# Linear attention in chunks of 64 tokens, with the state carried twice per tile and the query-value product in two banks by turns

## The chip, the cores and the metric

One Trainium2 chip, one of its cores. The metric is the device time of one execution in microseconds (us).

## The reference

Two layers in float32 on X of 2 x 2048 tokens with 256 channels, each added to its input. The first is a linear attention with 16 heads of 16 channels; the second a mixture of 32 experts with a shared one.

```python
K = X.reshape(B, L, H, d)                       # X is the normalised input
Q = rms_norm_multihead((X @ Wq.T).reshape(B, L, H, d), q_norm_w)
V = rms_norm_multihead((X @ Wv.T).reshape(B, L, H, d), v_norm_w)
W = jnp.cumsum(jnp.einsum('blhd,blhe->blhde', K, V), axis=1)
out = jnp.einsum('blhd,blhde->blhe', Q, W)      # token l sees all tokens up to l
# second layer: softmax over 32 experts, the best 4 of each token, swiglu of each, plus a shared swiglu
```

## The kernel before

The tokens are 32 tiles of 128, on 128 partitions. The kernel has three stages. The attention stage (about 20 to 215 us) computes the attention and, some tiles behind, the second norm, the routing and the scatter of the tokens to their experts. The expert stage (about 260 to 495 us) takes 144 blocks of tokens one after the other, and the end gathers and adds. The change is in the attention stage; in the part between the stages only banks of the shared expert's matmuls change places.

Each engine has its own program, unrolled by `pipelined(n, depth, step)`: iteration i calls `step`, and inside it `tile_of(s)` is tile i - s, so that the order of the statements in `step` is the order of that engine's instructions, with tiles of several ages mixed. Semaphores by name join the engines; `wait(eng, S[name], count)` blocks everything behind it on that engine.

What TensorE does for tile t, with its lines:
- L774 transposes the routed layer's input of an older tile, L785 the normalised input `xn` of a new one (into `xnT`), both into the bank `pT0`.
- L828 is the query-value product, `xnT` with `wqv`, 512 columns in two steps, into the bank `pQV`. ScalarE squares it (L571), VectorE sums, ScalarE and VectorE make the root (L594, L602, L1191 to L1216), and VectorE writes the normed queries `qn` (L1234) and values `vp` (L1240). The next product waits for both, since there is one bank.
- L817 transposes `qn` into `pT0`; ScalarE copies it as `qm` (four copies, L556) and `qT` (L562).
- L795 makes the scores: for each of 2 halves of the channels and each of 4 row groups of 32 channels, keys of 128 tokens against 256 columns (two heads' masks by 128 queries), into the four banks `pS`. VectorE multiplies three banks by the triangle `tri` (L1089), ScalarE copies the fourth (L527) and GpSimd cuts its triangle (L482).
- L869 is the product of the queries with the state `w_bd` carried from earlier tiles, a block-diagonal matrix, into `pO`. L877 adds the tile's keys and values to the state in `pT1`; VectorE writes it back as `w_bd` (L1180), once per tile. L888 adds the product of the masked scores with the values to `pO`. These three have 32 columns of weights each, in the four column groups.
- ScalarE scales `pO` into `oT` (L614), L803 transposes it, VectorE adds it to `xall` (L1113) and takes the statistics for the second norm.
- L838, L846, L847 and L858 belong to the routing and run every second tile.

GpSimd scatters the rows of a tile with four indirect DMAs (L467); SP's queue zeroes `ys` (L358) meanwhile.

Of the kernel before, what the change touches and what calls it, by code (L numbers as in the profile page):

```python
# [51 lines left out]
def build(nc, X, Wq, Wv, q_norm_w, v_norm_w, Wg, W1, W2, W3, Ws1, Ws2, Ws3, out):  # L52
# [12 lines left out]
    HB = P // 2  # L65
    NM = E // 2
# [21 lines left out]
    def banks_copied(t):  # L88
        return t

    def banks_masked(t):
        return 3 * t
# [25 lines left out]
    with ctx:  # L118
# [93 lines left out]
        s_sb = part(2048).rearrange("p (j g r l) -> p j g r l", j=4, g=2, r=2)  # L212
# [5 lines left out]
        xn = part(3 * 256).rearrange("p (b c) -> p b c", b=3)  # L218
# [43 lines left out]
        def tab_part(rows, width):  # L262
# [30 lines left out]
        pS = [pb(f"pS{j}") for j in range(4)]  # L293

        early = {(1, 0, 0): pQV, (1, 0, 1): pO, (1, 1, 0): pT1, (1, 1, 1): pS[0], (2, 0, 0): pS[2], (2, 0, 1): pS[1],
                 (2, 1, 0): pS[3], (2, 1, 1): pT1, (3, 0, 0): pS[2], (3, 0, 1): pS[3],
                 (3, 1, 0): pT0, (3, 1, 1): pQV}

        def h_bank(g, m, n):
# [5 lines left out]
            qn_done v_done qT_ps qm_done qT_done state_ps state_done scores_ps masked o1_ps o_ps oT_done  # L305
# [5 lines left out]
            xT_ps xT_done hb_ps sge_done ge_done gT_ps gT_done y_ps y_done parts_sum parts_copied half_sum added summed s_copied masked_pool padded w13_staged w2_staged y2_done kept""".split()  # L311
# [14 lines left out]
        DVE_CONSTS = 20  # L326
# [86 lines left out]
        def _(pool):  # L413
# [56 lines left out]
            def step(tile_of):  # L470
                if (a := tile_of(9)) is not None:
                    pool_wait(S["xr_done"], a.t + 1)
                    pool_wait(S["prob_done"], a.p + 1)
                    pool_wait(S["dest_done"], a.t + 1)
                    pool_wait(S["pos_done"], a.p + 1)
                    scatter(a, 0)
                if (a := tile_of(9)) is not None:
                    scatter(a, 1)
                if (a := tile_of(2)) is not None:
                    pool_wait(S["s_copied"], banks_copied(a.t) + 1)  # L480
                    v = s_sb[:, 1].rearrange("p g r l -> p (g r) l")
# [23 lines left out]
        def _(act):  # L505
# [3 lines left out]
            def normalise(t):  # L509
# [6 lines left out]
                wait(act, S["state_ps"], t - 2)  # L516
                act.activation(xn[:, t % 3, :], xall[:, t, :], ACT.Identity, bias=bias, scale=scale).then_inc(S["xn_done"], 1)
# [6 lines left out]
            def copy_scores(a, j):  # L524
                wait(act, S["scores_ps"], 4 * a.t + j + 1)
                wait(act, S["o_ps"], a.t)
                act.copy(s_sb[:, j].rearrange("p g r l -> p (g r l)"), pS[j][:]).then_inc(S["s_copied"], 1)  # L527

            def step(tile_of):
                if (a := tile_of(1)) is not None:  # L530
                    wait(act, S["xnT_ps"], a.t + 1)
                    wait(act, S["scores_ps"], 4 * (a.t - 2))
# [16 lines left out]
                if (a := tile_of(3)) is not None:  # L549
                    copy_scores(a, 1)  # L550
                if (a := tile_of(2)) is not None:
                    wait(act, S["qT_ps"], a.t + 1)
                    wait(act, S["scores_ps"], 4 * a.t)
                    for r in range(2):
                        for g in range(KC):
                            last = act.activation(qm[:, r, g, :], pT0[:, g * P:(g + 1) * P], ACT.Copy,  # L556
                                                  scale=mwq[:, r, g:g + 1])
                    last.then_inc(S["qm_done"], 1)
                if (a := tile_of(2)) is not None:
                    wait(act, S["qT_ps"], a.t + 1)  # L560
                    wait(act, S["o1_ps"], a.t - 1)
                    act.copy(qT[:, a.b], pT0[:, 0:D].rearrange("p (g m) -> p g m", g=KC)).then_inc(S["qT_done"], 1)  # L562
                if (a := tile_of(5)) is not None:
                    wait(act, S["nb2_done"], a.t + 1)
                    wait(act, scattered[a.r8], 64 * (a.t // 8))
                    act.activation(xr[:, a.r8, 0:D], xall[:, a.t, :], ACT.Identity, bias=nb[:, a.b, 0:1],
                                   scale=rr[:, (a.t + LAG) % 2, 2 * H:2 * H + 1]).then_inc(S["xr_done"], 1)
                if (a := tile_of(1)) is not None:
                    wait(act, S["qv_ps"], a.t + 1)
                    wait(act, S["ss_done"], a.t)  # L570
                    act.activation(sq, pQV[:], ACT.Square, scale=float(d) ** -0.5).then_inc(S["sq_done"], 1)  # L571
# [14 lines left out]
                if (a := tile_of(0)) is not None and a.t > 1:  # L586
                    normalise(a.t)
# [20 lines left out]
                if (a := tile_of(3)) is not None:  # L608
                    wait(act, S["o_ps"], a.t + 1)
                    wait(act, S["ot_ps"], a.t)  # L610
                    if a.t == 0:
                        act.wait_ge(S["wc_in"], 64)
                    for g in range(KC):
                        last = act.activation(oT[:, g, :], pO[:, g * P:(g + 1) * P], ACT.Copy, scale=wvc[:, g:g + 1])  # L614
                    last.then_inc(S["oT_done"], 1)
# [105 lines left out]
        def _(pe):  # L721
# [38 lines left out]

            def step(tile_of):
                if (a := tile_of(5)) is not None:
                    if a.t == NT - 3:
                        pe.wait_ge(S["masked"], banks_masked(NT))
                        pe.wait_ge(S["s_copied"], banks_copied(NT))
                        shared_half(0, 0, 0)
                    wait(pe, S["xr_done"], a.t + 1)
                    wait(pe, S["qT_done"], a.t + 4, NT)
                    wait(pe, S["qm_done"], a.t + 4, NT)
                    wait(pe, S["lg_done"], (a.t - 1) // 2)  # L770
                    wait(pe, S["rk_done"], (a.t - 2) // 2)
                    wait(pe, S["lgT_done"], a.t // 2)
                    for c in range(KC):
# [4 lines left out]
                    if a.t == NT - 1:  # L778
                        shared_half(0, 1, 1)
                if (a := tile_of(0)) is not None:  # L780
                    wait(pe, S["xn_done"], a.t + 1)
                    wait(pe, S["qT_done"], a.t - 1)
                    wait(pe, S["qm_done"], a.t - 1)
                    for g in range(KC):
                        last = pe.transpose(pT0[:, D + g * P:D + (g + 1) * P], xn[:, a.r3, g * P:(g + 1) * P], ident[:])  # L785
                    last.then_inc(S["xnT_ps"], 1)
                if (a := tile_of(2)) is not None:
# [3 lines left out]
                    wait(pe, S["masked"], banks_masked(a.t))  # L791
                    wait(pe, S["s_copied"], banks_copied(a.t))
                    for g in range(KC):
                        for j in range(4):
                            last = pe.matmul(pS[j][:, g * 256:(g + 1) * 256], xnT[32 * j:32 * j + 32, a.r3, g, :],  # L795
                                             qm[32 * j:32 * j + 32, :, g, :], start=(g == 0), stop=True,
                                             skip_group_check=True)
                            if g == KC - 1:
                                last.then_inc(S["scores_ps"], 1)
                if (a := tile_of(3)) is not None:  # L800
                    wait(pe, S["oT_done"], a.t + 1)
                    for g in range(KC):
                        last = pe.transpose(pO[:, D + g * P:D + (g + 1) * P], oT[:, g, :], ident[:])  # L803
                    last.then_inc(S["ot_ps"], 1)
                    if a.t == NT - 2:
                        pe.wait_ge(S["state_done"], NT - 1)
                        shared_half(1, 1, 0)
                    if a.t == NT - 1:
                        shared_half(0, 0, 1)
# [667 lines left out]
```

## Time and profile before

| | us |
|---|---|
| median of 3 runs | 559.55 (555.07 to 562.66) |
| the profiled execution | 559.33 |
| its span, first to last instruction | 557.4 |
| TensorE busy | 527.4 |
| VectorE, ScalarE, GpSimd busy | 382.2, 376.5, 331.8 |

The rows of the profile come from the one profiled execution. "Busy" is the time in which an engine has at least one instruction in work; TensorE's matmuls overlap each other, so their durations add up to more than the time that they take. PE is TensorE's matmuls, PEld its weight loads, DVE VectorE, ACT ScalarE, POOL GpSimd. A float32 matmul of the program is two matmul records and two weight loads in the trace.

### The profile page before, as it was taken

To read this page: it belongs to the slowest core of one execution; us is meant where nothing else is said; L and a number is where in the kernel's file an instruction comes from. 1 tells how busy PE (TensorE), PEld (TensorE's weight loads), DVE (VectorE), ACT (ScalarE), POOL (GpSimd) and SP (SyncE) were. 2 spreads that over 40 slices of the span, in tenths; PEclk is the share of its full clock that TensorE was granted. 3 is DMA by queue.
4 is the path that set the end of the run, shared out by engine and by line. 5 is a ranking of instruction groups with operands and counts; after the bars stand their busy time and mean duration, and the time that the engine had idled before them with its cause. 6 is when DMAs were issued, how large, how long until landed. Compare 5 with 4: busy or idle time off the path is not lost.

```text
span 557.4 us, 18176 instructions
## 1 busy us (share of the span) xinstructions
PE 527.4 (95%) x5177; PEld 383.1 (69%) x5177; DVE 382.2 (69%) x1354; ACT 376.5 (68%) x1258; POOL 331.8 (60%) x367
## 2 busy tenths in 40 slices
PE   6798999999999999699999999999999999997996
PEld 2355666666666665357998988999999995544554
DVE  7698999999999996664444444444444446744786
ACT  2687899988989985402766766777677776653452
POOL 6010377776777777771665555666666564446992
PEclk8999999999999999899999999999999999998999
DMA  8998355556456554954676776766666554428999
GB/s 259 316 292 264 125 217 211 187 215 227 186 198 246 188 192 152 366 194 127 195 219 201 221 225 199 214 193 194 194 193 198 180 187 145 143 79 342 408 409 347
DMA packets 65088, 123.29 MB, mean 221 GB/s; under 512 B 9824, under 2 KB 44000, under 8 KB 64992
## 3 DMA queue, kind: packets, MB, share of 16 engines
q1 hardware_dynamic: 47824, 78.07, 44.1%
q0 software_dynamic: 13056, 39.86, 19.2%
q10 hardware_dynamic: 4112, 4.19, 2.3%
q8 instruction: 45, 0.74, 0.6%
q14 instruction: 51, 0.42, 0.3%
HBM read 58.49 MB, written 63.60 MB: 219 GB/s over the span
## 4 chain that ended last, share of the span: by engine, by line
PE 79%; DMA 5%; DVE 4%; issue 4%; ACT 3%; POOL 2%; SPq 1%; ACTq 1%; DVEq 0%; POOLq 0%
PE pS L967 18%; PE pQV L828 10%; PE pS L985 9%; PE pS L741 8%; PE pS L795 5%; PE pO L888 5%; DMA xg<-xs 3%; PE pO L869 3%; PE pT L946 3%; PE pQV L946 2%; PE pQV L757 2%; PE pO L757 2%; PE pT L774 2%; PE pO L803 2%; PE pT L817 1%
## 5 line engine op out<-in xcount | busy, mean ns | idle before, releaser
L495 POOL DMA_INDIRECT ys<-gsh,dst x144 | 138.1, 959 | 108.3 <-ACT gsh L663 86.6
L467 POOL DMA_INDIRECT xs<-xg,posi x128 | 123.8, 967 | 52.1 <-issue 31.4
L967 PE MATMUL pS<-after_a,x2T_all 128*128 128x128 f32 x1024 | 135.5, 276 | 0.0
L967 PEld LDWEIGHTS pS<-after_a,x2T_all 128*128 128x128 f32 x1024 | 124.5, 192 | 0.0
L1375 DVE TENSOR_TENSOR after_a<-after_a,pS 128x128 f32<-128x128 f32 x144 | 41.5, 288 | 79.9 <-ACT after_a L651 76.1
L1346 DVE COPY x2T_all<-w 128x512 f32 x144 | 63.9, 444 | 32.9 <-issue 32.5
L985 PE MATMUL pS<-w,after_a 128*128 x256 | 76.7, 381 | 0.0
L1089 DVE TENSOR_TENSOR w<-pS,tri 128x512 f32<-128x512 f32 x96 | 65.1, 679 | 1.0 <-PE pS L795 1.0
L828 PE MATMUL pQV<-w 128*128 128x512 f32 x128 | 63.7, 621 | 0.5 <-ACT w L533 0.5
L663 ACT ACTIVATE gsh<-pS,xg 128x256 f32<-128x256 f32 x128 | 60.6, 474 | 0.4 <-issue 0.4
L662 ACT CAST dst<-xg 128x1 int32 x128 | 24.5, 191 | 45.3 <-PE pS L985 43.3
L741 PE MATMUL pS<-x2T_all,ws 128*128 128x512 f32 x104 | 50.6, 636 | 1.3 <-ACT sg L624 0.7
L651 ACT ACTIVATE after_a<-pS 128x128 f32<-128x128 f32 x144 | 40.1, 279 | 16.5 <-PE pS L967 10.7
L482 POOL TENSOR_SCALAR_AFFINE_SELECT w<-w 128x512 f32<-128x512 f32 x32 | 20.6, 643 | 43.3 <-ACT w L527 43.0
L500 POOL TENSOR_TENSOR w<-w 128x512 f32<-128x512 f32 x32 | 40.7, 1272 | 7.7 <-DMA w<-ys 7.4
L985 PEld LDWEIGHTS pS<-w,after_a 128*128 128x128 f32 x256 | 38.9, 192 | 0.4 <-issue 0.4
L556 ACT ACTIVATE w<-pT,mwq 128x128 f32<-128x128 f32 x128 | 36.8, 379 | 1.9 <-PE pT L817 1.7
L741 PEld LDWEIGHTS pS<-x2T_all,ws 128*128 128x128 f32 x104 | 20.9, 207 | 24.6 <-issue 24.3
L795 PE MATMUL pS<-w 32*128 32x256 f32 x512 | 36.7, 401 | 0.0
L828 PEld LDWEIGHTS pQV<-w 128*128 128x128 f32 x128 | 22.2, 194 | 20.2 <-issue 18.2
L888 PE MATMUL pO<-w 128*32 128x128 f32 x1024 | 34.6, 274 | 1.3 <-POOL w L482 0.6
L647 ACT COPY after_a<-pT 128x256 f32<-128x256 f32 x72 | 26.1, 363 | 11.4 <-PE pT L946 11.3
(221 smaller groups left out, 1019.8 us busy)
## 6 DMA issues: line engine op xcount, KB each, us to landing
xg<-xs SPq DMA_DIRECT2D x128, 160.0 KB, 2.8
ys<-gsh SPq DMA_DIRECT2D x32, 512.0 KB
w<-ys SPq DMA_DIRECT2D x32, 512.0 KB, 15.3
w<-in_L_ffn_W ACTq DMA_DIRECT2D x1, 4096.0 KB, 18.6
out<-xall SPq DMA_DIRECT2D x14, 256.0 KB, 7.2
xs<-padrow SPq DMA_DIRECT2D x32, 80.0 KB
xg<-xs SPq DMA_DIRECT2D x32, 80.0 KB, 2.2
ys<-gsh,dst POOLq DMA_INDIRECT x144
```

The lines of the kernel that those rows point to most:

```text
L467: pool.indirect_dma_start(out=xs, out_offset=bass.IndirectOffsetOnAxis(ap=posi[:, a.r8, k:k + 1], axis=0), in_=xr[:, a.r8, :], in_offset=N ...
L495: pool.indirect_dma_start(out=ys, out_offset=bass.IndirectOffsetOnAxis(ap=dst[:, j % 8:j % 8 + 1], axis=0), in_=y[:, j % 8, :], in_offset= ...
L663: act.activation(y[:, a.r8, :], pS[2 + a.b][:, 0:D], ACT.Copy, scale=xg[:, a.r8, bass.ds(e[0] + D, 1)]).then_inc(S["y_done"], 1)
L741: last = pe.matmul(h_bank(g, m, n)[:], ws13[:, k, n, m * P:(m + 1) * P], x2T_all[:, k, g * TG:(g + 1) * TG], start=(k == 0), stop=(k == KC ...
L795: last = pe.matmul(pS[j][:, g * 256:(g + 1) * 256], xnT[32 * j:32 * j + 32, a.r3, g, :], qm[32 * j:32 * j + 32, :, g, :], start=(g == 0), ...
L828: last = pe.matmul(pQV[:], xnT[:, a.r3, k, :], wqv[:, k, :], start=(k == 0), stop=(k == KC - 1))
L888: last = pe.matmul(pO[32 * j:32 * j + 32, g * P:(g + 1) * P], vp[:, a.b, 4 * g + j, r:r + 2, :], s_sb[:, j, g, r, :], start=False, stop=(r ...
L967: last = pe.matmul(pS[a.b][:, n * P:(n + 1) * P], w13_staged(a.t)[:, (2 * k + n) * F:(2 * k + n + 1) * F], xgT[:, a.b, k, :], start=(k == ...
L985: last = pe.matmul(pS[2 + a.b][:, 0:D], geT[:, a.b, :], w2_of(e), start=True, stop=True)
L1089: dve.tensor_tensor(s_sb[:, j].rearrange("p g r l -> p (g r) l"), pS[j][:].rearrange("p (n l) -> p n l", l=P), tri[:].unsqueeze(1).to_broa ...
L1346: dve.tensor_copy(w13_staged(j), w13[:, bass.ds(staged_of(j), 1), :, :, :].rearrange("p a k n f -> p (a k n f)")).then_inc(S["w13_staged"], 1)
L1375: dve.tensor_tensor((ge if mixed(a.t) else geT)[:, a.b, :], sge[:, a.b, :], pS[a.b][:, F:2 * F], ALU.mult).then_inc(S["ge_done"], 1)
```

## The change

A tile's 128 tokens are treated as two chunks of 64 (`CH`). Scores are made only between tokens of one chunk; what a chunk needs of the one before comes through the state, which is therefore carried twice per tile.

- Scores: 16 matmuls of 128 columns with 64 columns of weights each, instead of 8 of 256 columns with 128. They fill half of each bank. VectorE masks them with two instructions over two banks each; ScalarE's copy and GpSimd's cut are gone.
- Query times state: 16 matmuls of 64 columns over 64 partitions, instead of 8 of 128 columns over 128. The halves of the block-diagonal state that hold zeros are left out.
- State: `add_to_state` runs for each chunk (8 matmuls over 64 partitions each), and `carry_state` on VectorE writes 128 instead of 256 columns, twice.
- Scores times values: 32 matmuls of 64 columns over 64 partitions, instead of 16 of 128 over 128, behind a new wait for query times state.
- The query-value product alternates between `pQV` and `pO` and is issued in two parts, with the transposes of `qn` between them. The attention's output moves into the free halves of `pS` (`pO_chunks`), the transposes of `qn` and `oT` too.
- The transposes of `oT` stand behind the query-value product; `normalise` and the copy to `xr` stand ahead of `qm` on ScalarE; `vp` is written at the start of VectorE's next iteration; `xn` has four buffers.

The core of the diff:

```diff
 TensorE
                 if (a := tile_of(2)) is not None:
                     wait(pe, S["qm_done"], a.t + 1)
+                    wait(pe, S["qT_done"], a.t + 1)
+                    wait(pe, S["oT_done"], a.t)
+                    wait(pe, S["x2_done"], a.t - 1)
                     for g in range(KC):
-                        for j in range(4):
-                            last = pe.matmul(pS[j][:, g * 256:(g + 1) * 256], xnT[32 * j:32 * j + 32, a.r3, g, :],
-                                             qm[32 * j:32 * j + 32, :, g, :], start=(g == 0), stop=True,
+                        for c in range(2):
+                            for j in range(4):
+                                last = pe.matmul(pS[j][c * CH:(c + 1) * CH, g * P:(g + 1) * P],
+                                                 xnT[32 * j:32 * j + 32, a.r3, g, c * CH:(c + 1) * CH],
+                                                 qm[32 * j:32 * j + 32, :, g, c * CH:(c + 1) * CH],
...
+                if (a := tile_of(0)) is not None:
+                    wait(pe, S["xnT_done"], a.t + 1)
+                    wait(pe, S["qn_done"], a.t - 1)
+                    wait(pe, S["v_done"], a.t - 1)
+                    pe.matmul((pQV, pO)[a.b][:], xnT[:, a.r3, 0, :], wqv[:, 0, :], start=True, stop=False)
                 if (a := tile_of(1)) is not None:
                     wait(pe, S["qn_done"], a.t + 1)
+                    wait(pe, S["masked"], scores_masked(a.t - 1) + 1)
                     for g in range(KC):
+                        last = pe.transpose(pQT[:, g * P:(g + 1) * P], qn[:, a.b, g * P:(g + 1) * P], ident[:])
                 if (a := tile_of(0)) is not None:
+                    pe.matmul((pQV, pO)[a.b][:], xnT[:, a.r3, 1, :], wqv[:, 1, :], start=False, stop=True).then_inc(S["qv_ps"], 1)
+                if (a := tile_of(3)) is not None:
+                    wait(pe, S["oT_done"], a.t + 1)
...
                 if (a := tile_of(2)) is not None:
                     wait(pe, S["qT_done"], a.t + 1)
+                    wait(pe, S["carried"], states_summed(a.t, 1))
+                    wait(pe, S["masked"], scores_masked(a.t + 1))
                     for g in range(KC):
+                        for turn in range(2):
+                            for j in range(4):
+                                i = j // 2
+                                c = (i + turn) % 2
+                                last = pe.matmul(pO_chunks[32 * j:32 * j + 32, c, g, :], carry(a.b, c)[i * CH:(i + 1) * CH, g, j % 2, :],
+                                                 qT[i * CH:(i + 1) * CH, a.b, g, c * CH:(c + 1) * CH],
                     last.then_inc(S["o1_ps"], 1)
                 if (a := tile_of(2)) is not None and a.t < NT - 1:
+                    add_to_state(a, 1)
                 if (a := tile_of(2)) is not None:
+                    pe.wait_ge(S["o1_ps"], a.t + 1)
                     for g in range(KC):
                         for r in range(2):
+                            for c in range(2):
+                                for j in range(4):
+                                    last = pe.matmul(pO_chunks[32 * j:32 * j + 32, c, g, :],
+                                                     vp[c * CH:(c + 1) * CH, a.b, 4 * g + j, r:r + 2, :],
+                                                     s_sb[c * CH:(c + 1) * CH, j, g, r, :],
                     last.then_inc(S["o_ps"], 1)
+                if (a := tile_of(1)) is not None:
+                    add_to_state(a, 0)
 VectorE
+            def mask_scores(a, half):
+                banks = slice(2 * half, 2 * half + 2)
...
+            def carry_state(t, c):
...
+                    dve.tensor_tensor(carry(t % 2, c),
+                                      pT1[:, 0:KC * 2 * d].rearrange("p (g e) -> p g e", g=KC).unsqueeze(2).to_broadcast([P, KC, 2, 2 * d]),
+                                      head_mask[:, :, 0:CH].rearrange("p g (j e) -> p g j e", j=2), ALU.mult).then_inc(S["carried"], 1)
 ScalarE
-                if (a := tile_of(3)) is not None:
-                    copy_scores(a, 1)
+                if (a := tile_of(0)) is not None and a.t > 1:
+                    normalise(a.t)
 GpSimd
-                    pool.affine_select(out=v, in_=v, compare_op=ALU.is_ge, fill=0.0, base=0,
-                                       pattern=[[0, 4], [1, P]], channel_multiplier=-1).then_inc(S["masked_pool"], 1)
```

## Rows read from the trace of the kernel before

**Rows 1.** The page: busy us (share) of the engines; instruction queue: packets, MB, share.
```profile
...
PE 527.4 (95%) x5177; PEld 383.1 (69%) x5177; DVE 382.2 (69%) x1354; ACT 376.5 (68%) x1258; POOL 331.8 (60%) x367
...
q8 instruction: 45, 0.74, 0.6%
```

**Rows 2.** Windows: us, busy time (xcount) by engine, granted clock, DMA share, GB/s.
```profile
...
20.30:215.00 194.70, 191.63 (x3068) 124.30 (x3072) 184.27 (x754) 169.97 (x570) 115.90 (x131) 1.00 0.61 214
26.30:56.13 29.83, 28.24 (x438) 17.57 (x438) 26.20 (x84) 24.49 (x73) 3.17 (x5) 1.00 0.92 276
100.30:198.04 97.74, 97.55 (x1572) 63.92 (x1568) 94.73 (x407) 88.81 (x305) 72.07 (x81) 1.00 0.56 207
```

**Rows 3.** Chain that ended last, 112 to 126 us, shares by line.
```profile
...
by line: PE pQV L828 26.9%; PE pS L795 19.8%; PE pO L888 17.6%; PE pT L774 7.9%; PE pO L869 7.2%; PE pO L803 5.3%; PE pT L785 4.7%; PE pT L817 4.2%; PE pT L858 2.5%; PE pT L877 1.8%; PE pT L846 1.4%; PE pT L838 1.2%; PE pT L847 0.2%
```

**Rows 4.** TensorE in order of time, one steady tile: start, us, line.
```profile
...
184.28 0.62 PE L869 MATMUL pO<-w,w_bd 128*32 128x128 f32 x16
184.71 0.31 PE L877 MATMUL pT<-w 128*32 128x32 f32 x16
184.84 1.06 PE L888 MATMUL pO<-w 128*32 128x128 f32 x32
185.83 0.44 PE L774 MATMUL pT<-ident,xg 128*128 128x128 f32 x2
...
186.41 1.14 PE L795 MATMUL pS<-w 32*128 32x256 f32 x16
187.49 0.44 PE L803 MATMUL pO<-ident,w 128*128 128x128 f32 x2
```

**Rows 5.** TensorE in order of time around 42 and 50 us.
```profile
...
41.55 0.62 PE L869 MATMUL pO<-w,w_bd 128*32 128x128 f32 x11
43.26 0.31 PE L869 MATMUL pO<-w,w_bd 128*32 128x128 f32 x3 [1.08 <-issue]
...
49.45 0.28 PE L888 MATMUL pO<-w 128*32 128x128 f32 x1
...
50.20 0.64 PE L888 MATMUL pO<-w 128*32 128x128 f32 x16 [0.47 <-issue]
```

**Rows 6.** Queue q8 in the windows 40.6:41.9, 47.4:48.7 and 53.2:54.4.
```profile
...
q8 instruction: 1, 0.02, 5.8%
...
q8 instruction: 1, 0.02, 5.7%
...
q8 instruction: 1, 0.02, 5.2%
```

**Rows 7.** Groups of VectorE and ScalarE, 100 to 198 us: busy us, mean ns.
```profile
...
L1089 DVE TENSOR_TENSOR w<-pS,tri 128x512 f32<-128x512 f32 x48 | 32.6, 678 | 0.0
...
L1180 DVE TENSOR_TENSOR w_bd<-pT,head_mask 128x256 f32<-128x256 f32 x16 | 6.5, 404 | 0.0
...
L614 ACT ACTIVATE w<-pO,wvc 128x128 f32<-128x128 f32 x32 | 9.7, 352 | 0.0
L527 ACT COPY w<-pS 128x512 f32<-128x512 f32 x16 | 9.4, 589 | 2.2 <-PE pS L795 2.2
```

**Rows 8.** Queue q8 in 100.3:198.04, 127.3:128.5, 156.1:157.2 and 186.8:187.9.
```profile
...
q8 instruction: 13, 0.21, 1.0%
...
q8 instruction: 1, 0.02, 5.0%
...
q8 instruction: 1, 0.02, 5.3%
...
q8 instruction: 1, 0.02, 6.0%
```

**Rows 9.** Windows between three turns of the instruction queue.
```profile
...
124.42:154.79 30.37, 30.31 (x489) 19.84 (x484) 29.92 (x130) 27.25 (x93) 22.04 (x25) 1.00 0.57 211
154.79:184.95 30.16, 30.08 (x491) 19.63 (x485) 28.80 (x125) 27.76 (x98) 22.62 (x26) 1.00 0.57 212
```

More of the change, by code:

```diff
@@ L522, in _ @@
                 act.copy(wqv[:, k, :], (pT0, pT1)[k][:]).then_inc(S["wt_done"], 1)
[L524 to L527, printed above, removed]
             def step(tile_of):
@@ L561, in step @@
                     wait(act, S["o1_ps"], a.t - 1)
[L562 to L567, printed above, removed]
+                    act.copy(qT[:, a.b], pQT.rearrange("p (g m) -> p g m", g=KC)).then_inc(S["qT_done"], 1)
                 if (a := tile_of(1)) is not None:
@@ L585, in step @@
                     act.copy(lgT[:], pT0[:, 0:P]).then_inc(S["lgT_done"], 1)
-                if (a := tile_of(0)) is not None and a.t > 1:
-                    normalise(a.t)
+                if (a := tile_of(3)) is not None:
+                    wait(act, S["o_ps"], a.t + 1)
+                    wait(act, S["ot_ps"], a.t)
+                    if a.t == 0:
+                        act.wait_ge(S["wc_in"], 64)
+                    for g in range(KC):
+                        last = act.activation(oT[:, g, :].rearrange("p (c l) -> p c l", c=2), pO_chunks[:, :, g, :], ACT.Copy,
+                                              scale=wvc[:, g:g + 1])
+                    last.then_inc(S["oT_done"], 1)
                 if (a := tile_of(1, LAG)) is not None:
@@ L759, in shared_z, with add_to_state @@
                     last.then_inc(S["z_ps"], 1)
+            def add_to_state(a, c):
+                wait(pe, S["v_done"], a.t + 1)
+                wait(pe, S["carried"], states_summed(a.t, c))
+                for g in range(KC):
+                    for j in range(4):
+                        last = pe.matmul(pT1[32 * j:32 * j + 32, g * 2 * d:(g + 1) * 2 * d],
+                                         xn[c * CH:(c + 1) * CH, a.r4, g * P + 32 * j:g * P + 32 * j + 32],
+                                         vp[c * CH:(c + 1) * CH, a.b, 4 * g + j, 0:3:2, :],
+                                         start=(a.t % NTB == 0 and c == 0 and g == 0), stop=True, skip_group_check=True)
+                last.then_inc(S["state_ps"], 1)
             def step(tile_of):
@@ L871, in step @@
                     last.then_inc(S["o1_ps"], 1)
                 if (a := tile_of(2)) is not None and a.t < NT - 1:
-                    wait(pe, S["v_done"], a.t + 1)
-                    wait(pe, S["state_done"], a.t)
-                    for g in range(KC):
-                        for j in range(4):
-                            last = pe.matmul(pT1[32 * j:32 * j + 32, g * 2 * d:(g + 1) * 2 * d],
-                                             xn[:, a.r3, g * P + 32 * j:g * P + 32 * j + 32], vp[:, a.b, 4 * g + j, 0:3:2, :],
-                                             start=(a.t % NTB == 0 and g == 0), stop=True, skip_group_check=True)
@@ L1135, in step @@
                     stats1(n.t)
+                if (a := tile_of(4)) is not None:
+                    wait(dve, S["ot_ps"], a.t + 1)
+                    dve.tensor_tensor(xall[:, a.t, :], xall[:, a.t, :], pOT, ALU.add).then_inc(S["x2_done"], 1)
+                if (a := tile_of(4)) is not None:
+                    wait(dve, S["x2_done"], a.t + 1)
+                    dve.bn_stats(st2[:], xall[:, a.t, :]).then_inc(S["stats2"], 1)
+                if (a := tile_of(4)) is not None:
+                    wait(dve, S["stats2"], a.t + 1)
+                    dve.bn_aggr(mv2[:, a.t % 8, :], st2[:]).then_inc(S["mean2"], 1)
                 if (a := closing(tile_of(8))) is not None:
@@ L1148, in step @@
                                           ).then_inc(S["var2_done"], 1)
+                if (a := tile_of(3)) is not None and a.t < NT - 1:
+                    carry_state(a.t + 1, 0)
                 if (a := tile_of(1)) is not None:
```

203 lines of the change are left out of this document (87 added, 116 removed).

## The prediction

> **What bounds the kernel now.** I read the page first: TensorE is busy for 95% of the span, VectorE and ScalarE for 69% and 68% [rows 1]. Shares over the whole span mix stages, so the second view is the windows over the attention stage, 20.3 to 215.0 us: TensorE is busy for 191.6 of 194.7 us at the full 2.4 GHz, 6.08 us for each of the 32 tiles, and 16 tiles of its steady part take 97.7 us, 6.11 us each. VectorE is busy for 94.7 of these and ScalarE for 88.8, so both sit close behind [rows 2]. The chain of waits over two tiles of that part consists of TensorE lines alone [rows 3], and the sequence of its groups shows no hole in a steady tile: each group starts as soon as the one before has streamed [rows 4]. So what the change saves on TensorE is worth its time until VectorE, or something that the busy shares don't show, comes next.
>
> There is such a thing. TensorE has two holes in the middle of an unbroken burst of matmuls, where no wait stands in the code: after the eleventh record of a group of L869 it stops until 43.26, and after the first of a group of L888 until 50.20. Both are released by "issue" [rows 5]. In the queue view of the same moments a packet of the kind "instruction" on q8 runs just before each: the first lies inside 40.6 to 41.9 and the second inside 47.4 to 48.7 (5.8% and 5.7% of 16 engines for 1.3 us are 1.2 us each) [rows 6]. In both cases TensorE goes on 1.4 to 1.5 us after the packet ends. q8 carries 45 packets and 0.74 MB [rows 1], 16.4 KB a packet, against TensorE's 10,354 matmul and weight-load records: one packet for 230 records. I read this so: TensorE's instructions come in pieces of 16 KB, the next piece is asked for when the one before it is entered, and if it lands late, TensorE stands still.
>
> **The change part by part, on TensorE.** A float32 matmul gives two matmul records and two weight loads.
> Scores (L795): 16 records of 256 columns take 1.08 us [rows 4], four at a time in the four row groups. They become 32 records of 128 columns in tiles of 32 x 64. If eight run at once these are four rounds. Sixteen records of 128 columns, four at a time, take 0.43 us at L869 [rows 4], so a round takes 0.11 us; with the 0.2 us that L795 has beyond its own streaming the group takes 0.64 us, and saves 0.44.
> Product of scores and values (L888): 32 records of 128 columns take 0.99 us [rows 4]. They become 64 of 64 columns, eight at a time: 8 rounds of 0.055 are 0.44, with the 0.11 of the change of shape 0.55. Saved 0.44.
> Query times state (L869): 32 records of 64 columns, four at a time, 8 x 0.055 = 0.44: nothing saved.
> State: twice per tile instead of once, 0.13 us more [rows 4].
> The new wait on o1_ps ahead of the value product (L888's successor): a small matmul needs some 0.2 us from start to end (the group of L877 lasts 0.31 and the next group starts 0.13 after it [rows 4]), and the restart I estimate at 0.1; the state group covers 0.12. I take 0.25 us, bounds 0.1 and 0.5. Behind it on the queue stand the second product, the state group and the next tile's transposes, and ScalarE's copy oT waits for it.
> Sum: 6.11 - 0.44 - 0.44 + 0.13 + 0.25 = 5.6 us a tile. The two banks let the first half of the query-value product go ahead of qn, which costs no columns; since TensorE has no hole there now, they gain nothing by themselves, but they keep the norm chain from becoming the limit.
>
> The Trainium skill (TensorE: Matmul & The Clock Gate, section Wait — 56ns, not 53.3ns?) says that start to start of matmuls never falls below about 25 ns. The trace differs: the 16 records of L877 take 0.13 us from the group's start to the next group's. By the page the 160 matmul records of the four groups would take 4.0 us and the change would lose about 1.4 us a tile on this alone.
>
> **The other engines.** VectorE is busy 94.7/16 = 5.92 us a tile. It loses one of three masks of 678 ns and has two state products of half the size for one of 404 ns; 128 columns lie between nothing and 404, I take 0.27: 5.92 - 0.68 + 0.14 = 5.38. ScalarE loses the copy of 589 ns, from 5.55 to 4.96 [rows 2, 7]. GpSimd loses its mask and keeps its scatters; it is busy for only 72.1 of 97.7 us [rows 2]. The moved steps (normalise and the copy to xr before qm, x2's statistics behind the second mask, the transposes of oT behind the query-value product) issue nothing new; the product of the next tile waits for oT, since both use banks 2 and 3, and beside the end of the value product (0.2), ScalarE's two copies of 352 ns [rows 7] and the restart (0.1) stand some 0.9 us of state group and transposes: cover for all but 0.1. No DMA is moved. The fourth buffer of xn only loosens a wait. So by engines alone the tile would take 5.65 to 5.7 us, and the stage 32 x 0.42 = 13 us less.
>
> **The term that decides: TensorE's instructions.** Scores, query times state, state and scores times values have 160 matmul and load records a tile now and 320 after. At 196 records a tile (3,140 in 16 tiles [rows 2]) and 13 packets in these 98 us [rows 8] a packet holds 241 of them, the rest of it being semaphore instructions; 0.81 packets a tile. The 160 new ones add no waits and count with the bytes of an instruction alone: 16.4 KB over some 256 instructions, 0.63 packets. So 0.81 + 0.63 = 1.44 packets a tile, and over the stage 6,140/241 = 25.5 packets [rows 2] become 45.5.
> A packet now has 97.7/13 = 7.5 us. At 5.65 us a tile it would have 3.9 us. What does it need? From the turn at which it is asked for to the time at which its instructions can be used:
> - With the DMA engines full (share 0.92 from 26 to 56 us [rows 2]): from the restart at 43.26 to that at 50.20, 6.9 us; then from 50.20 to the packet inside 53.2 to 54.4 [rows 6], with 1.45 us behind it, 5.5 us.
> - In the steady part, counting on from those two holes (which are one packet apart), the turns fall at 124.42, 154.79 and 184.95, four packets and 973 and 976 records apart, all in L888 [rows 9], where TensorE's queue holds little time. Their packets lie in windows that end at 128.5, 157.2 and 187.9 [rows 8]. With 1.45 us: 5.5, 3.85 and 4.4 us, mean 4.6. The sequencer is ahead of the matmuls by part of a group, which I estimate at 0.1 to 0.3 us. I take 4.75; bounds 4.1 (the mean of the two short ones) and 5.5.
> If only one piece is under way at a time, a tile then takes 1.44 x 4.75 = 6.8 us instead of 6.1, and TensorE waits for instructions in the middle of its bursts. The stage: 45.5 x 4.75 = 216 us, and some five packets up to 57 us take 6.9 instead of 4.75, 11 more: 227 us against 194.7. Nothing after the stage changes except its start. The profiled execution took 559.3 us (span 557.4), within 0.3 us of the median of 559.55, so 559 + 32 = 591 us.
>
> The Trainium skill (Runtime: NRT & Kernel Launch, section Instruction fetch mechanics) says that instructions come in blocks of 16 KiB, 256 instructions, that the next is fetched while the current one runs and that this is mostly hidden; it gives TensorE a store of 2,048 instructions and elsewhere speaks of two lines only. The trace agrees with the blocks, and its two holes speak for the two lines.
>
> **Rivals.**
> 1. The instructions arrive in time (they are asked for further ahead than I read, or in under 3.9 us). Then the engines decide: 5.65 us a tile, 559.3 - 13 = 546 us, 540 to 552. For it: only two holes in 45 packets, both where the DMA engines were full. Against: both end 1.4 to 1.5 us behind a packet, and no stretch of the trace asks for a packet in under 6.5 us. By the Trainium skill's store of 2,048 instructions this is how it would go. Chance 0.20.
> 2. The packets take about 4 us: 45.5 x 4.0 = 182 and 11, with long and short turns that don't even out some 5 more: 198 us, 562; it meets "no change". Chance 0.14.
> 3. Tiles don't run eight at a time, only rows or only columns as now: no saving of 0.88, the tile at 6.11 + 0.13 + 0.25 = 6.5 us and the time at 571 us if instructions are in time. The trace has no group that splits both. Chance 0.06.
> 4. My forecast, 591 us; with 4.1 us a packet 45.5 x 4.1 + 11 = 198 and 562, with 5.5 261 and 625. Chance 0.60.
>
> **How the numbers follow.** The time is that of the fourth case. Slower by over 2% (above 570.7; 2% is about what a measurement here tells from no change): 0.52 of the forecast's 0.60, 0.02 of the second case, 0.04 of the third, and a little for packets slower than I saw: 0.62. Within 2%: 0.17. Faster by over 2% (under 548.4): 0.21, from the first case with the low end of the second. The range must reach down to the first case and up to some 5.2 us a packet: 544 to 612. By itself the forecast's own range is 562 to 625.
>
> **What would show it.** q8 with about 65 packets instead of 45, about 4.5 to 5 us apart in the stage; TensorE busy for clearly less than 98% of it, with holes of 1 us and more put down to "issue" in L869's, L877's and L888's successors and in the scores, with VectorE and ScalarE waiting for TensorE. The scores at 0.64 us and the value product at 0.55 where no hole cuts them show the savings; a gap of 0.25 us ahead of the value product shows the new wait. I am wrong if packets come 4 us apart or less without such holes: then the tile is at 5.65 us and VectorE is the next limit. I am also wrong if the holes at 41.9 and 49.5 had a cause of their own.

## The result: 13% slower, and the profile after

The changed kernel takes 634.39 us (median of 4 runs, 632.48 to 637.40) against 560.70: a ratio of 1.134, with a 95% interval of 1.124 to 1.144. The forecast had the sign and the limit, the supply of TensorE's instructions, and was 43 us short; its range ended at 612.

The profiled execution took 637.4 us with a span of 635.7. From its page: busy time of the engines, TensorE's clock and the DMA share in 40 slices, the instruction queue, and the chain.

```profile
span 635.7 us, 23229 instructions
...
PE 552.9 (87%) x7737; PEld 394.1 (62%) x7737; DVE 379.9 (60%) x1356; ACT 361.5 (57%) x1226; POOL 310.8 (49%) x335
...
PEclk8868997889898888888799999999999999999899
DMA  8993234343533433334935667676666665435999
...
q8 instruction: 66, 1.08, 0.8%
...
PE 66%; issue 11%; DVE 7%; SPq 5%; ACT 4%; DMA 4%; POOL 1%; ACTq 1%; DVEq 0%; POOLq 0%
```

TensorE has 2,560 more matmul records (7,737 against 5,177 [rows 1]), 80 for each tile, and as many more weight loads; q8 brings 66 packets instead of 45, where the prediction said 65. "Issue", waiting for nothing that the profile shows, is 11% of the chain. The clock row has changed in the first half: many slices are at 0.8. Two windows, the attention stage and a steady part of it:

```profile
20.30:297.00 276.70, 222.49 (x5671) 139.13 (x5670) 184.88 (x781) 160.50 (x557) 100.05 (x104) 0.90 0.45 156
...
100.00:250.00 150.00, 122.96 (x3250) 78.31 (x3241) 107.01 (x467) 94.22 (x330) 69.06 (x72) 0.91 0.42 156
```

TensorE was busy for 98% of the stage before [rows 2] and is for 80% of it now; VectorE and ScalarE have fallen too, to 67% and 58%. A tile has 356 matmul and load records now (196 and 160), so the 6,491 records of the second window are 18.2 tiles, 8.2 us each instead of 6.1. The last value product of the stage starts at 286.63 us instead of 214.47: 72 of the 78 us by which the span grew lie in the stage.

The waits of TensorE over the stage (waited for, us in total, times, longest):

```profile
PE pS L805 <- issue: 14.5, 10, 4.8
PE pS L890 <- issue: 13.7, 7, 2.6
PE pS L821 <- DVE w L1100: 7.4, 12, 1.6
PE pT L763 <- issue: 6.1, 3, 2.5
```

All rows with "issue" together are 37.5 us in 26 holes; before there were 1.6 us in 2 [rows 5]. One of them in order of time (L805 scores, L890 value product):

```profile
92.11 0.48 PE L805 MATMUL pS<-w 32*64 32x128 f32 x16 [0.49 <-issue]
...
96.09 0.68 PE L890 MATMUL pS<-w 64*32 64x64 f32 x42
99.40 0.54 PE L890 MATMUL pS<-w 64*32 64x64 f32 x19 [2.63 <-issue]
```

The value product stops after its 42nd record, where the code has no wait. In the queue view of the window 95.9:97.99 there is one instruction packet (4.8% of 16 engines for 2.09 us, 1.6 us):

```profile
q8 instruction: 1, 0.02, 4.8%
```

The packet ends at 97.97, and TensorE goes on 1.4 us later, the same delay as at the two holes of the kernel before [rows 5, 6]. The hole before this one ended at 92.11. Between the two restarts lie 7.3 us and 256 instructions (counted in the trace: matmuls, weight loads, and those of the sequencer, such as waits). The count holds for the stage: from 34.75 to 265.09 us each of 21 restarts from a hole of 0.3 us or more lies 256 instructions, or a multiple of that, behind the one before.

The 7.3 us are not typical. The packet that follows the restart at 99.40 is in the window from 101 to 102.1 us:

```profile
q8 instruction: 1, 0.02, 5.3%
```

It ends at 102.00. With the same 1.4 us behind it, its instructions could be used 4.0 us after that restart. From 57 to 270 us the trace has 18 restarts for which this time can be read. For the 8 in the scores it is 6.0 to 7.3 us, for the 10 in the value product, the state's sum and the transposes of `xn` 3.9 to 5.0 us; the mean is 5.35 us. Why the packet comes later after a restart in the scores is not shown.

The same groups with no hole in them, from 135.6 and from 141.1 us on (L763 is the state's sum for the next tile):

```profile
135.60 0.69 PE L805 MATMUL pS<-w 32*64 32x128 f32 x32
136.23 2.08 PE L814 MATMUL pO<-w 128*128 128x512 f32 x2
...
138.52 1.56 PE L828 MATMUL pO<-w 128*128 128x512 f32 x2
139.92 0.38 PE L834 MATMUL pS<-ident,w 128*128 128x128 f32 x2
...
141.14 1.14 PE L890 MATMUL pS<-w 64*32 64x64 f32 x64
142.10 0.33 PE L763 MATMUL pT<-w 64*32 64x32 f32 x16
142.50 0.41 PE L781 MATMUL pT<-ident,xg 128*128 128x128 f32 x2
...
143.46 0.70 PE L805 MATMUL pS<-w 32*64 32x128 f32 x32 [0.33 <-ACT w L590]
144.30 1.12 PE L814 MATMUL pQV<-w 128*128 128x512 f32 x2
145.75 0.41 PE L821 MATMUL pS<-ident,w 128*128 128x128 f32 x2 [0.33 <-DVE w L1100]
145.99 1.02 PE L828 MATMUL pQV<-w 128*128 128x512 f32 x2
146.85 0.38 PE L834 MATMUL pS<-ident,w 128*128 128x128 f32 x2
```

Four things can be read here. The scores take 0.63 us, as the forecast's eight tiles at once gave. The value product takes 0.96 us here (141.14 to 142.10) and the state's sum behind it 0.40, where the forecast had 0.55 and 0.13. The half of the query-value product at L828 takes 0.86 us from start to the next start in the second tile and 1.40 in the first, which follows the hole of 2.5 us that ended at 134.68; L814 needs 2.08 us instead of 1.12. The window from 134.6 to 144.4 us shows why:

```profile
134.60:144.40 9.80, 9.11 (x221) 5.92 (x221) 5.29 (x24) 5.49 (x20) 7.45 (x8) 0.83 0.48 174
```

A granted clock of 0.83 is a third of these 9.8 us at 1.2 GHz and the rest at 2.4. And L821 waits for VectorE's first mask (L1100), a wait that the change added and that the prediction passed over.

### The profile page after: what moved, and what is told of

It reads as the page before. It is cut to its first block, busy times and chain, and to the rows that moved or that the text cites. A ratio compares the mean times of both kernels' runs of the same rounds, so it can differ in the third digit from the quotient of the medians.

```text
span 635.7 us, 23229 instructions
## 1 busy us (share of the span) xinstructions
PE 552.9 (87%) x7737; PEld 394.1 (62%) x7737; DVE 379.9 (60%) x1356; ACT 361.5 (57%) x1226; POOL 310.8 (49%) x335
## 3 DMA queue, kind: packets, MB, share of 16 engines
q8 instruction: 66, 1.08, 0.8%
## 4 chain that ended last, share of the span: by engine, by line
PE 66%; issue 11%; DVE 7%; SPq 5%; ACT 4%; DMA 4%; POOL 1%; ACTq 1%; DVEq 0%; POOLq 0%
PE pS L975 14%; PE pS L738 7%; PE pS L993 6%; PE pS L890 5%; PE pS L805 3%; DMA xg<-xs 3%; PE pO L814 3%; PE pS L878 2%; PE pQV L814 2%; PE pQV L828 2%; PE pO L828 2%; SPq L392 2%; PE pQV L754 2%; PE pQV L954 2%; PE pS L821 2%
## 5 line engine op out<-in xcount | busy, mean ns | idle before, releaser
L559 ACT ACTIVATE w<-pS,mwq 128x128 f32<-128x128 f32 x128 | 36.5, 368 | 33.9 <-PE pS L821 32.9
L1100 DVE TENSOR_TENSOR w<-pS,tri 128x512 f32<-128x512 f32 x64 | 43.6, 682 | 15.6 <-PE pS L805 15.4
L590 ACT ACTIVATE w<-pS,wvc 128x128 f32<-128x128 f32 x64 | 20.0, 363 | 52.5 <-PE pS L890 52.5
L805 PE MATMUL pS<-w 32*64 32x128 f32 x1024 | 29.1, 318 | 18.2 <-issue 14.5
L890 PE MATMUL pS<-w 64*32 64x64 f32 x2048 | 32.4, 229 | 14.1 <-issue 13.7
L503 POOL TENSOR_TENSOR w<-w 128x512 f32<-128x512 f32 x32 | 40.6, 1270 | 8.1 <-DMA w<-ys 7.8
L890 PEld LDWEIGHTS pS<-w 64*32 64x32 f32 x2048 | 25.0, 107 | 18.7 <-issue 15.4
L805 PEld LDWEIGHTS pS<-w 32*64 32x64 f32 x1024 | 18.9, 150 | 26.9 <-issue 26.9
L763 PE MATMUL pT<-w 64*32 64x32 f32 x1008 | 28.2, 199 | 6.5 <-issue 6.1
```

The lines of the kernel that those rows point to most:

```text
L503: pool.tensor_tensor(parts(t)[:, 0:2, :], parts(t)[:, 0:2, :], parts(t)[:, 2:4, :], ALU.add).then_inc(S["parts_sum"], 1)
L805: last = pe.matmul(pS[j][c * CH:(c + 1) * CH, g * P:(g + 1) * P], xnT[32 * j:32 * j + 32, a.r3, g, c * CH:(c + 1) * CH], qm[32 * j:32 * j ...
L890: last = pe.matmul(pO_chunks[32 * j:32 * j + 32, c, g, :], vp[c * CH:(c + 1) * CH, a.b, 4 * g + j, r:r + 2, :], s_sb[c * CH:(c + 1) * CH, ...
L1100: dve.tensor_tensor(s_sb[:, banks].rearrange("p j g r l -> p j (g r) l"), pS_all[:, banks, 0:4 * CH].rearrange("p j (n l) -> p j n l", l=C ...
```

## Experiments

Theory 1: TensorE's instructions come in packets of 256, the next one asked for when the last one's turn begins; the change needs 1.44 packets a tile instead of 0.81, and that sets its time. Theory 2: the new order, the new waits and the smaller tiles do, and the number of instructions doesn't matter.

**160 more records per tile and nothing else (b_split_all).** The kernel before, each matmul of the four groups cut in two by columns; shown for L888, the other three alike:

```diff
-                            for j in range(4):
-                                last = pe.matmul(pO[32 * j:32 * j + 32, g * P:(g + 1) * P],
-                                                 vp[:, a.b, 4 * g + j, r:r + 2, :], s_sb[:, j, g, r, :],
+                            for c in range(2):
+                                for j in range(4):
+                                    last = pe.matmul(pO[32 * j:32 * j + 32, g * P + c * HB:g * P + (c + 1) * HB],
+                                                     vp[:, a.b, 4 * g + j, r:r + 2, :], s_sb[:, j, g, r, c * HB:(c + 1) * HB],
```

> The kernel before with one thing changed: each matmul of the four groups L795, L869, L877 and L888 is split in two by columns, so that TensorE streams the same columns in the same shapes of tile with 160 more matmul and load records per tile, as many as the change adds. Results are the same. Theory 1 (TensorE's instructions don't come in fast enough): 1.44 packets of q8 per tile at about 5.7 us, as measured in the changed kernel, 8.2 us a tile, so 615 to 645 us and about 65 packets, with holes put down to issue. Theory 2 (the new order, the new wait and the smaller tiles cost the time, the instruction count doesn't matter): within 1% of the kernel before, 555 to 566 us.

Measured: 627.58 us, ratio 1.119 (1.114 to 1.124). The same columns in the same order cost 67 us, nine tenths of what the change costs, once they are cut into twice as many matmuls and weight loads. Its page, a window and TensorE's waits from 100 to 250 us:

```profile
q8 instruction: 65, 1.06, 0.8%
```

```profile
100.00:250.00 150.00, 128.19 (x3176) 91.94 (x3175) 112.43 (x460) 101.82 (x340) 80.83 (x90) 0.91 0.42 155
```

```profile
PE pO L893 <- issue: 12.4, 7, 3.3
PE pS L796 <- issue: 8.3, 5, 2.1
```

There are 42.3 us of such holes over its stage, and the clock falls as in the changed kernel. Not all of the 67 us is supply. Where no hole cuts them, the four groups take longer too: at the median of the trace the scores 1.10 instead of 1.08 us, L871 and L881 together 0.85 instead of 0.56, L893 1.22 instead of 1.01. That is 0.5 us a tile, an estimated 17 us of the stage. Theory 2 is out as the main cause.

**64 more (b_split_888).** Only L888 cut.

> The kernel before with only L888 split in two by columns: 64 more records per tile, the same columns, the same results. 0.81 + 0.25 = 1.06 packets per tile; at 6.1 us a tile a packet has 5.75 us. Theory 1: near the point at which supply begins to bind; since the turns are uneven some holes appear, 565 to 585 us, much less than two fifths of the loss of the full split. Theory 2: 558 to 563 us.

Measured: 575.49 us, 1.026 (1.021 to 1.031), with 12.4 us of holes and 53 packets. Two fifths of the instructions cost under a quarter of the time: holes begin somewhere near one packet a tile of 6 us. The cut value product itself takes 1.24 us instead of 1.01 at the median, an estimated 7 of the 15 us.

**64 fewer than the change (a_half_value).**

```diff
-                        for r in range(2):
+                        for r in range(1):
                             for c in range(2):
                                 for j in range(4):
                                     last = pe.matmul(pO_chunks[32 * j:32 * j + 32, c, g, :],
```

> The changed kernel with the product of scores and values only for r = 0: the second half of the heads of each pair is left out of it. 64 records fewer per tile. Theory 1: 1.44 - 0.25 = 1.19 packets of 5.7 us, 6.8 us a tile instead of 8.2: 585 to 600 us. Theory 2: only the columns left out are saved, 0.33 us a tile: 620 to 625 us.

Measured: 600.61 us, 1.073 (1.067 to 1.080), at the upper end of theory 1. Half of the value product was left out, 0.3 us a tile or 10 us by the expectation's estimate, and 34 us went.

**The same number less with the same results (a_merged).** 64 fewer records, by larger matmuls in two groups:

```diff
-                            for j in range(4):
-                                i = j // 2
+                            for i in range(2):
                                 c = (i + turn) % 2
-                                last = pe.matmul(pO_chunks[32 * j:32 * j + 32, c, g, :], carry(a.b, c)[i * CH:(i + 1) * CH, g, j % 2, :],
+                                last = pe.matmul(pO_chunks[CH * i:CH * i + CH, c, g, :],
+                                                 carry(a.b, c)[i * CH:(i + 1) * CH, g, :, :].rearrange("p j e -> p (j e)"),
...
-                    for j in range(4):
-                        last = pe.matmul(pT1[32 * j:32 * j + 32, g * 2 * d:(g + 1) * 2 * d],
+                    for i in range(2):
+                        last = pe.matmul(pT1[CH * i:CH * i + CH, g * CH:(g + 1) * CH],
```

> The changed kernel with the same results and the same chunks, but with two of its groups in larger matmuls: query times state takes the 64 x 64 block-diagonal state as one weight (8 matmuls instead of 16), and the state's sum takes 64 channels against 64 columns (4 per chunk instead of 8; the mask drops the cross terms). 64 records fewer per tile, some 0.2 us of columns fewer, one or two more changes of shape. Theory 1 (instruction supply): 1.19 packets a tile, like the kernel without half of the value product, 592 to 604 us. Theory 2 (order and waits alone): 626 to 636 us.

Measured: 605.50 us, 1.083 (1.078 to 1.087); just above the range for theory 1 and far from that for theory 2. Two different edits that take away 64 records come within 5 us of each other.

**128 fewer (a_few).** The value product loops over one g and one r, the state's sum over one g.

> The changed kernel with the product of scores and values only for g = 0, r = 0, and the sum of the state only for g = 0: both are left out for the rest. 128 records fewer per tile, 0.94 packets per tile, all engines' other work and all waits kept. Theory 1: supply no longer binds; the tile comes to what the engines need, 5.3 to 5.7 us, so 540 to 552 us, under the kernel before. Theory 2: only columns are saved, 0.6 us a tile: 612 to 618 us.

Measured: 577.37 us, 1.033 (1.025 to 1.041). Of the 74 us of the change 57 have gone, but both theories missed: I had said 540 to 552. With 50 packets there are 4.9 us of holes left. What remains is seen in TensorE's waits, 100 to 198 us, some 16 tiles:

```profile
PE pS L821 <- DVE w L1100: 7.2, 15, 0.9
PE pT L763 <- DVE w_bd L1114: 4.9, 15, 0.5
```

Both waits are the change's own. The transposes of qn (L821) now write a bank of `pS` and so wait until VectorE has masked it; the state's sum for the next tile (L763) waits until VectorE has carried the state that the group of the same tile has just made. They are 0.76 us a tile.

**Late transposes (a_few_late).** The block of L821 moved behind the second half of the product.

> The changed kernel with 128 records fewer per tile (value product only for g = 0 and r = 0, state's sum only for g = 0, as before), and in addition with the transposes of qn behind both halves of the query-value product instead of between them. In the run without this move TensorE waits in each tile for VectorE's first mask ahead of these transposes (L821), 0.5 us on average. If that wait is what keeps the tile at 6.3 us, the second half of the product (0.87 us) covers it: 558 to 566 us. If the loop through VectorE's queue is the limit and the wait only shows its slack, another wait takes its place: 572 to 580 us.

Measured: 569.69 us, 1.019 (1.015 to 1.023), 8 us less and between the two expectations. The transposes no longer wait for the mask; other waits have grown in its place (again 100 to 198 us):

```profile
PE pT L763 <- DVE w_bd L1114: 6.4, 14, 0.7
PE pS L878 <- DVE w L1100: 2.1, 7, 0.3
```

**VectorE relieved (a_few_light).** The masks cut to a quarter:

```diff
-                dve.tensor_tensor(s_sb[:, banks].rearrange("p j g r l -> p j (g r) l"),
+                dve.tensor_tensor(s_sb[:, banks, 0, 0, :], pS_all[:, banks, 0:CH],
```

> The kernel with 128 records fewer per tile and late transposes of qn, which came to 570 us, with VectorE's two masks cut to the scores that the left-out product still reads (64 of 256 columns of each bank; the rest is not masked). VectorE is relieved of about 0.9 us a tile, all waits stay. If VectorE's queue sets the tile of 6.15 us there: down to 5.4 to 5.7 us, 546 to 556 us. If it is a loop of waits with idle VectorE in it, the two shorter masks in the loop still shorten it a little: 560 to 568 us.

Measured: 565.15 us, 1.006 (1.002 to 1.010). This fits the loop of waits. VectorE's throughput is not the floor: in the window it has 15 us to spare and the time falls by 5 us only.

```profile
100.00:198.00 98.00, 83.70 (x1851) 53.60 (x1850) 82.73 (x412) 83.41 (x294) 62.47 (x66) 1.00 0.57 212
```

TensorE, VectorE and ScalarE are all busy for 84 to 85% of it; in the two kernels with full masks VectorE was busy for 92 to 93%. So with instructions enough the chunked order stands at 565 to 577 us by waits among three engines, none of which is full, even with three quarters of the value product left out. Which loop closes last was not separated further.

**The complete change with late transposes (a_late).**

> The changed kernel complete, with only the transposes of qn moved behind both halves of the query-value product. With few instructions this move gained 7.7 us. If the instruction supply sets the time of the changed kernel, a wait less gains nothing: 629 to 638 us. If the order and the waits do: 620 to 627 us.

Measured: 629.10 us, 1.121 (1.115 to 1.127): at the low end of what theory 1 allowed. The move that gains 8 us with few instructions gains 5 with all of them.

**Why does a packet take so long? (b_split_nz and the control b_nz)**

```diff
-                sp.dma_start(ys_rows[:, n, :], zero).then_inc(S["ys_zeroed"], 16)
+                sp.dma_start(ys_rows[:, n, 0:16], zero[:, 0:16]).then_inc(S["ys_zeroed"], 16)
```

> The kernel before with all four groups split in two by columns (160 more records per tile), and with SP's 32 zeroing transfers of 512 KB cut to 8 KB each, so that most of ys is not zeroed. Theory A (the instruction packets wait behind the bulk traffic on the DMA engines, so the supply is slow because of it): packets come some 0.5 to 1 us sooner, 585 to 608 us. Theory B (the time from asking to using is a fixed latency): 622 to 630 us.

> Control for the run above: the kernel before with the zeroing transfers cut to 8 KB each. TensorE has no waits for instructions to lose but the two near 42 and 50 us; both theories: 555 to 562 us.

Measured: 609.72 us, 1.087 (1.081 to 1.093), against 627.58 with all transfers; the control 560.21, 1.001 (0.998 to 1.004). With the zeroing cut 18 of the 67 us are gone, and nothing in the kernel that has instructions enough. That lies between the two theories' ranges, nearer to A: the zeroing traffic delays the packets, but the larger part of their time stays. From 100 to 198 us, first without and then with the zeroing:

```profile
q8 instruction: 18, 0.29, 1.4%
...
100.00:198.00 98.00, 86.66 (x2255) 62.30 (x2257) 81.95 (x336) 72.07 (x241) 56.48 (x63) 0.97 0.27 90
```

```profile
q8 instruction: 17, 0.28, 1.3%
...
100.00:198.00 98.00, 85.55 (x2136) 61.88 (x2135) 75.06 (x309) 68.19 (x228) 51.95 (x58) 0.91 0.42 155
```

The DMA share is 0.27 instead of 0.42, the packets are 5.4 us apart instead of 5.8, and the granted clock is 0.97 instead of 0.91 with shorter holes. From a restart to 1.4 us after the next packet's end the means are 4.7 and 5.1 us (57 to 290 us, 16 and 20 restarts). In both kernels the next packet starts 1.1 to 2.0 us after a restart in the value product, and in half of the cases or more 4.0 to 4.6 us after one in the scores: that late start is not the zeroing's doing, and its cause stays open.

**Fewer instructions in the kernel before (b_merged).**

```diff
-                        for j in range(4):
-                            at = g * P + 32 * j
-                            last = pe.matmul(pO[32 * j:32 * j + 32, g * P:(g + 1) * P], w_bd[:, a.b, at:at + 32], qT[:, a.b, g, :],
+                        last = pe.matmul(pO[:, g * P:(g + 1) * P], w_bd[:, a.b, g * P:(g + 1) * P], qT[:, a.b, g, :],
...
-                        for j in range(4):
-                            last = pe.matmul(pT1[32 * j:32 * j + 32, g * 2 * d:(g + 1) * 2 * d],
+                        for i in range(2):
+                            last = pe.matmul(pT1[HB * i:HB * i + HB, g * HB:(g + 1) * HB],
```

> The kernel before, same results, with fewer TensorE instructions: query times state takes each 128 x 128 block-diagonal state as one weight (2 matmuls instead of 8, the same time of streaming) and the state's sum takes 64 channels against 64 columns (4 instead of 8; the mask drops the cross terms). 40 records fewer per tile. If supply costs the kernel before only its two holes near 42 and 50 us: 1 to 3 us faster, 556 to 560 us. If many small delays of the kernel before are supply too: 545 to 555 us.

Measured: 566.97 us, 1.011 (1.007 to 1.016): 1.1% slower, both expectations missed. It has 41 packets and not one hole put down to issue in its stage. In order of time:

```profile
156.43 0.66 PE L867 MATMUL pO<-w,w_bd 128*128 128x128 f32 x4
157.02 0.45 PE L875 MATMUL pT<-w 128*64 128x64 f32 x8
157.40 1.08 PE L887 MATMUL pO<-w 128*32 128x128 f32 x32
```

Query times state takes 0.59 us with 4 records of full width, against 0.43 with 16 narrow ones [rows 4], and the state's sum 0.38 against 0.13. Four narrow ones side by side are done sooner than one wide one. The Trainium skill (TensorE: Matmul & The Clock Gate, section LDWEIGHTS (loading the stationary operand)) says that a load takes its time by the columns of the weights; this trace agrees in so far as a pair of load and matmul of 128 columns took 0.15 us here and a round of four narrow ones, with 32 columns of weights each, 0.11.

No version with 64-token chunks came under the kernel before, so none is offered as better than both.

## Why the prediction was right in kind and wrong in size

**Right: the limit.** "The term that decides" was the instruction supply. The count (65 packets forecast, 66 seen), the delay from packet to restart (1.4 us) and the holes in the middle of bursts came as said, and the split kernel shows the cause without the change. Rival 1, by which the instructions arrive in time, is out, and with it the reading of a store of 2,048 instructions; the Trainium skill (Runtime: NRT & Kernel Launch, section Instruction fetch mechanics) calls the fetch mostly hidden, and the kernels here with 1.2 packets a tile and more show the opposite. Rival 3 is out: the scores take 0.63 us.

**Wrong: the step "a tile then takes 1.44 x 4.75", which made the stage 45.5 x 4.75.** In the changed kernel 27 packets fall in the 150 us from 100 to 250 us:

```profile
q8 instruction: 27, 0.44, 1.3%
```

That is 5.6 us a packet; 45.5 x 5.6 is 255 us for the stage where I had 216, and this alone is 39 of the 43 us. It is not that a packet needs so much longer than I took. The trace has 37 turns from 60.98 to 265.09 us, one every 256 instructions. Timed as I had timed my three, from TensorE's start on a turn to 1.4 us after the end of the packet that follows, they need 4.7 us on average. But 4.75 is the mean need of a turn, not the time between turns. A turn lasts as long as its packet needs or as long as TensorE itself takes for 256 instructions, whichever is more, and the turns are uneven. Of the 36 intervals between these turns 17 ended in a hole and took 5.2 us, just what their packets needed; the other 19 took 6.1 us with a need of 4.3. The dense turns wait, and the turns that span the query-value product, a wait or a stretch at the lower clock do not give the time back. I had an allowance for this, 5 us, in rival 2 only.

My three turns were also a narrow sample, all in L888, with 3.7 to 5.4 us. All 19 turns of the kernel before from 57 to 200 us have a mean of 5.1 us and reach from 3.7 to 7.7; they were there to be counted. The 6.9 us between its two restarts, which I put down to full DMA engines alone, have their like in the 7.3 us from 92.11 on, where the DMA share was 0.46.

**Missing: the clock.** I wrote of no term for it. The granted clock is 0.90 of full over the stage, so TensorE ran at the lower level for a fifth of 277 us, 55 us. If half of that is lost, as the groups at both levels suggest (1.40 against 0.86 us), it is at most some 25 us; with each line's records at the lower level counted at their own time at the full one, it is 22. With the 36 us of added holes and the 10 to 17 us by which the chunked order stands behind the kernel before where instructions suffice, that makes 68 to 78 us for the measured 74. This is a second account of the same 74 us, by what TensorE did, and not to be added to the one by turns: the lower clock lengthens turns and is in the 5.6 us. Both are worked out from rows, and the share of the clock was not isolated by a run.

**Wrong: 5.65 us a tile by engines alone.** Rival 1's 546 us rested on this; the runs gave 577, 570 and 565 us with less work than the complete change. Two things failed. The first is the sum of the groups. At the median of the whole groups at the full clock the scores take 0.63 us as I said, but query times state with the state's first sum, and the new wait behind them, take 0.74, and the value product with the second sum 1.15. That is 2.52 us where I had 2.14 (0.64, 0.44, 0.26, 0.55 and 0.25) and where the kernel before has 2.65. So the change saved 0.13 us a tile in these groups instead of 0.5. Why 64 records of 64 columns take longer than their eight at a time gave is not shown. The second is the sentence on the moved steps: I named the wait of the scores for oT, but not that qn's transposes, now in a bank of `pS`, wait for a mask, nor that the second state sum waits for VectorE in the same tile.

## What to carry to other kernels

Count instructions, not only columns: splitting float32 matmuls into narrower tiles keeps their columns and doubles their instructions. Here holes began at about one packet of 256 instructions per 6 us, and cutting DMA traffic made them shorter. And where a limit acts piece by piece, add up the longer of the two times for each piece; the mean of the one against the mean of the other hides the pieces that wait. The queue of instruction packets in the profile, beside holes put down to "issue" in the middle of a burst, shows it before any change is made. When outputs move into another group's bank, list the new pairs of writer and reader: each is a wait.

## What the runs showed of the hardware that I had not expected

- TensorE restarted 1.3 to 1.5 us after the end of an instruction packet in each of the 18 holes followed, always at a multiple of 256 instructions from the last. From a restart until the next packet's instructions could be used it took from 3.9 us (82.39) to 7.3 us (92.11, 257.84).
- The granted clock was 0.90 on average in a stage in which TensorE is busy for 80% of the time: from 57 us on every stretch at 1.2 GHz began between 0.8 us before and 1.7 us after TensorE went on from a hole or a wait of 1.2 to 3.0 us. With somewhat shorter holes in the split kernel the clock was 0.97 instead of 0.91.
- Full-width float32 matmuls of 128 columns take 0.15 us each back to back, four narrow ones beside each other 0.11 us a round: fewer instructions for the same product can be slower.
